# Mixture-of-experts stage: first weights split behind the weighing of the tile two back, and ahead of a one-tile expert's second weights

## What is computed

```
logits = flat @ router_w.T;  topk_w, topk_ids = top_k(softmax(logits), 4)
xs = rows of flat, sorted by expert            # 4096 tokens x 4 choices
gu = ragged_dot(xs, w1, group_sizes)           # w1: 32 x 1024 x 1024
act = silu(g) * u
ys = ragged_dot(act, w2, group_sizes)          # w2: 32 x 512 x 1024
routed = sum over the 4 choices of weight * ys
out = residual + routed + silu(flat @ sg) * (flat @ su) @ sd
```

## Time and profile before

| | |
|---|---|
| Median of three runs | 4691.68 us (4690.73 to 4694.3) |
| The profiled execution, its own time | 4695.12 us |
| Its span, first to last instruction | 4693.4 us |
| Mean granted TensorE clock | 0.978 |
| PE busy | 4473.3 us |
| DVE busy | 2569.9 us |
| ACT busy | 1795.0 us |
| POOL busy | 703.4 us |

### The profile page before, as it was taken

The page is one execution under the profiler, slowest core; times in us unless marked ns, Lnnn a source line. Parts: engine busy times, 40 slices in busy tenths (PEclk is TensorE's granted clock), DMA queues, the critical chain, the costliest instruction groups (busy, mean ns, idle before and its releaser), DMA issues.

```text
span 4693.4 us, 60863 instructions
## 1 busy us (share of the span) xinstructions
PE 4473.3 (95%) x19860; PEld 3545.8 (76%) x19863; DVE 2569.9 (55%) x2765; ACT 1795.0 (38%) x2596; POOL 703.4 (15%) x934
## 2 busy tenths in 40 slices
PE   6677999999999999999999999999999999999998
PEld 2245877777777777878888887887888878888787
DVE  8999999999999653433333434444341243333432
ACT  5665555555555332222222323334231242222321
POOL 1000000000000017111111111111111111111111
PEclk8888999999999999999999999999999999999999
DMA  6664866767676766654344545555452264444532
GB/s 227 248 255 177 292 237 249 261 225 272 246 264 232 263 219 185 242 180 114 99 127 112 165 116 161 169 163 188 141 170 58 59 202 128 112 112 116 161 108 62
DMA packets 247927, 835.08 MB, mean 178 GB/s; under 512 B 28160, under 2 KB 61056, under 8 KB 222976
## 3 DMA queue, kind: packets, MB, share of 16 engines
q1 hardware_dynamic: 172944, 572.77, 34.0%
q0 software_dynamic: 47728, 160.07, 15.4%
q10 hardware_dynamic: 27136, 100.67, 5.6%
HBM read 652.40 MB, written 181.01 MB: 178 GB/s over the span
## 4 chain that ended last, share of the span: by engine, by line
PE 85%; DVE 8%; issue 3%; ACT 3%; DMA 1%; DVEq 0%; ACTq 0%; POOL 0%; SPq 0%; POOLq 0%
PE ps L1545 35%; PE ps L1409 24%; PE ps L1559 17%; PE ps L1478 3%; PE ps L1431 1%; PE ps L1534 1%; DVE work L925 1%; DVE work L931 1%; PE ps L1419 1%; PE ps L1429 1%; DMA out<-work 1%; DVE work L952 1%; DVE work L954 1%; DVE work L935 1%; DVE work L958 1%
## 5 line engine op out<-in xcount | busy, mean ns | idle before, releaser
L1545 PE MATMUL ps<-halves 128*128 128x512 f32 x7152 | 1700.8, 394 | 25.8 <-DVE halves L1304 22.3
L1545 PEld LDWEIGHTS ps<-halves 128*128 128x128 f32 x7152 | 1340.0, 189 | 303.7 <-DVE halves L1304 24.4
L1409 PE MATMUL ps<-halves 128*128 128x512 f32 x6144 | 1451.5, 396 | 12.3 <-issue 12.3
L1409 PEld LDWEIGHTS ps<-halves 128*128 128x128 f32 x6144 | 1155.3, 189 | 285.7 <-issue 47.4
L1559 PE MATMUL ps<-halves 128*128 128x512 f32 x3576 | 834.9, 389 | 1.3 <-DVE halves L1324 1.3
L1559 PEld LDWEIGHTS ps<-halves 128*128 128x128 f32 x3576 | 671.2, 188 | 140.8 <-DVE halves L1324 1.6
L1308 DVE TENSOR_TENSOR halves<-ps,halves 128x1024 fp32r<-128x1024 f32 x150 | 183.6, 1224 | 884.4 <-ACT halves L807 884.4
L1304 DVE TENSOR_TENSOR halves<-work,halves 128x1024 fp32r<-128x1024 f32 (+1 forms) x320 | 440.5, 1433 | 114.9 <-ACT halves L811 114.9
L807 ACT ACTIVATE halves<-ps 128x1024 fp32r<-128x1024 f32 x150 | 154.0, 1027 | 849.6 <-PE ps L1545 849.6
L811 ACT ACTIVATE halves<-work 128x1024 fp32r<-128x1024 f32 (+1 forms) x320 | 369.7, 1221 | 96.3 <-PE ps L1559 66.5
L1324 DVE TENSOR_TENSOR halves<-ps,halves 128x256 fp32r<-128x256 f32 x298 | 112.3, 418 | 494.8 <-ACT halves L839 494.8
(11 more groups left out here) (186 smaller groups left out, 3787.8 us busy)
## 6 DMA issues: line engine op xcount, KB each, us to landing
halves<-split_dram SPq DMA_DIRECT2D x512, 512.0 KB, 5.6
work<-expert_w SPq DMA_DIRECT2D x192, 1024.0 KB, 5.7
split_dram<-halves ACTq DMA_DIRECT2D x32, 1024.0 KB, 4.9
plain<-shared_w SPq DMA_DIRECT2D x32, 512.0 KB, 3.2
gated_dram<-work ACTq DMA_DIRECT2D x32, 512.0 KB, 4.2
work<-side_t ACTq DMA_DIRECT2D x32, 512.0 KB, 5.5
work<-x_t ACTq DMA_DIRECT2D x32, 512.0 KB, 3.3
ratio_dram<-work ACTq DMA_DIRECT2D x32, 512.0 KB, 5.0
```

Of the source, the lines that this page charges most:

```text
L1409: last = pe.matmul(bank(k % 4), w, op[:, part], start=(c == 0 and w is w_hi and op is hi), stop=(c == CB - 1 and w is w_lo))
L1545: last = pe.matmul(ps_h[:, a * 512:a * 512 + 512], xp[:, xk * P:(xk + 1) * P], wp[:, rhs], start=(xk == 0 and xp is xhi and wp is whi[q]), ...
```

## The change

ACT and DVE use a new loop, `expert_loop_split`, in which `head` is taken apart into `first_weights`, `second_weights` and `rest` (a tile without its weighing). PE keeps `expert_loop`. The order on ACT and DVE becomes:

- expert e with more than one tile: `rest` of its first tile, its second weights, its other tiles, then the weighing of the tile two before the next expert's first, then the first weights of expert e+1. Before, those first weights came ahead of that weighing. Expert 0 ends in the same way.
- expert e with one tile: `rest` of its tile, then the first weights of expert e+1, then the weighing, then its own second weights. Before: its own second weights, the first weights of expert e+1, the weighing.

The counters of the splits are divided into one for first and one for second weights (8 and 2 steps for each expert) so that the two can be waited for in either order, on SP and PE too. DVE waits at the end of its opening tile until the last stores of the stage before have landed (`o_out`).

```diff
--- before.py
+++ after.py
@@ -28,7 +28,7 @@
...
-PIECES = 10
+W1, W2 = 8, 2
...
@@ -303,6 +303,48 @@
...
+        def expert_loop_split(eng, opening, weigh, rest, first_weights, second_weights, close):
+
+
+            def tile(g, j):
+                if not (isinstance(g, int) and g < 2):
+                    weigh(g - 2)
+                rest(g, j)
+
+            eng.wait_ge(s["cols_set"], 1)
+            opening(0)
+            tile(1, 0)
+            end0 = eng.value_load(cuts[0:1, 0:1], min_val=0, max_val=ROUTED_TILES - 2) + 2
+            with eng.If(end0 > 2):
+                with eng.Fori(2, end0) as g:
+                    tile(g, 0)
+            weigh(end0 - 2)
+            first_weights(1, end0)
+
+            with eng.Fori(1, EXPERTS - 1) as e:
+                first = eng.value_load(cuts[0:1, ds(e - 1, 1)], min_val=0, max_val=ROUTED_TILES - 2) + 2
+                end = eng.value_load(cuts[0:1, ds(e, 1)], min_val=1, max_val=ROUTED_TILES - 2) + 2
+                rest(first, e)
+                with eng.If(first + 1 < end):
+                    second_weights(e, first)
+                    with eng.Fori(first + 1, end) as g:
+                        tile(g, e)
+                    weigh(end - 2)
+                    first_weights(e + 1, end)
+                with eng.Else():
+                    first_weights(e + 1, end)
+                    weigh(end - 2)
+                    second_weights(e, first)
+            last = EXPERTS - 1
+            first = eng.value_load(cuts[0:1, last - 1:last], min_val=0, max_val=ROUTED_TILES - 2) + 2
+            end = eng.value_load(cuts[0:1, last:last + 1], min_val=1, max_val=ROUTED_TILES - 2) + 2
+            rest(first, last)
+            second_weights(last, first)
+            with eng.If(first + 1 < end):
+                with eng.Fori(first + 1, end) as g:
+                    tile(g, last)
...
@@ -475,7 +517,10 @@
...
-                    sp.wait_ge(s["w_lo"], (j - 1) * PIECES + (2 * q + 3 if q < 4 else q + 6))
+                    if q < 4:
+                        sp.wait_ge(s["w1_lo"], (j - 1) * W1 + (2 * q + 3))
+                    else:
+                        sp.wait_ge(s["w2_lo"], (j - 1) * W2 + (q - 2))
...
@@ -849,19 +894,18 @@
...
-            def tile(g, j):
-                if not (isinstance(g, int) and g < 2):
-                    weigh(g - 2)
+            def rest(g, j):
                 split_act(g - 1, 0)
                 split_act(g - 1, 1)
                 silu(g, 0)
                 split_x(g + 1)
                 silu(g, 1)
 
-            def head(g, j):
+            def first_weights(j, g):
                 for q in range(4):
                     split_weights(j, q, g)
-                tile(g, j)
+
+            def second_weights(j, g):
                 split_weights(j, 4, g)
                 split_weights(j, 5, g)
...
@@ -871,7 +915,7 @@
...
-            expert_loop(sc, opening, head, tile, close)
+            expert_loop_split(sc, opening, weigh, rest, first_weights, second_weights, close)
...
@@ -1300,8 +1344,12 @@
...
             def split_part_lo(j, q, i):
                 part = parts(q)[i]
-                ve.wait_ge(s["w_hi"], j * PIECES + (2 * q + i + 1 if q < 4 else q + 5))
-                ve.tensor_tensor(wlo[q][:, part], staged(q, part), whi[q][:, part].bitcast(f32), ALU.subtract).then_inc(s["w_lo"], 1)
+                if q < 4:
+                    ve.wait_ge(s["w1_hi"], j * W1 + (2 * q + i + 1))
+                else:
+                    ve.wait_ge(s["w2_hi"], j * W2 + (q - 3))
+                ve.tensor_tensor(wlo[q][:, part], staged(q, part), whi[q][:, part].bitcast(f32), ALU.subtract)\
+                    .then_inc(s["w1_lo" if q < 4 else "w2_lo"], 1)
...
@@ -1333,20 +1381,20 @@
...
-
-            def tile(g, j):
-                if not (isinstance(g, int) and g < 2):
-                    weigh(g - 2)
+                ve.wait_ge(s["o_out"], 16 * HALVES * CB + 1)
+
+            def rest(g, j):
                 split_act(g - 1, 0)
                 split_act(g - 1, 1)
                 gate_up(g, 0)
                 split_x(g + 1)
                 gate_up(g, 1)
 
-            def head(g, j):
+            def first_weights(j, g):
                 for q in range(4):
                     split_weights(j, q)
-                tile(g, j)
+
+            def second_weights(j, g):
                 split_weights(j, 4)
                 split_weights(j, 5)
...
@@ -1356,7 +1404,7 @@
...
-            expert_loop(ve, opening, head, tile, close)
+            expert_loop_split(ve, opening, weigh, rest, first_weights, second_weights, close)
...
@@ -1538,7 +1586,7 @@
...
-                        pe.wait_ge(s["w_lo"], j * PIECES + (2 * q + k // 2 + 2))
+                        pe.wait_ge(s["w1_lo"], j * W1 + (2 * q + k // 2 + 2))
...
@@ -1550,7 +1598,7 @@
...
-                    pe.wait_ge(s["w_lo"], j * PIECES + (q + 10))
+                    pe.wait_ge(s["w2_lo"], j * W2 + (q + 2))
```

More of the change, by code:

```diff
@@ L209, in adaln_moe @@
             "a_hi_s a_lo_s o_tr o_copy o_out prep prep_act masks rt rt_act rt_mask rt_pe cnt_copy "
-            "fill_set fill_out add_idx_set apart entry_ready listed_in slots_in cols_set w_hi w_lo w1_read w2_read "
+            "fill_set fill_out add_idx_set apart entry_ready listed_in slots_in cols_set w1_hi w1_lo w2_hi w2_lo w1_read w2_read "
             "rows_in row_idx_set x_tr x_hi x_lo silu_done act_done a_tr a_hi a_lo y_hi y_lo y_out zero_set "
@@ L218, in adaln_moe @@
         ONE_AHEAD = (
-            "o_tr o_copy o_out gated w_lo num ratio ratio_out gated_out a_tr w1_read w2_read act_done x_lo y_lo y_hi"
+            "o_tr o_copy o_out gated w1_lo w2_lo num ratio ratio_out gated_out a_tr w1_read w2_read act_done x_lo y_lo y_hi"
         ).split()
@@ L305, in expert_loop @@
                         tile(g, e)
+            close(eng.value_load(cuts[0:1, EXPERTS - 1:EXPERTS], min_val=1, max_val=ROUTED_TILES - 2) + 1)
+        def expert_loop_split(eng, opening, weigh, rest, first_weights, second_weights, close):
[34 more added lines that the diff above has]
+                    tile(g, last)
             close(eng.value_load(cuts[0:1, EXPERTS - 1:EXPERTS], min_val=1, max_val=ROUTED_TILES - 2) + 1)
@@ L810, in split_part_hi @@
                 sc.wait_ge(w_in[q], (j + 1) * 16)
-                sc.activation(whi[q][:, part], staged(q, part), ACT.Copy).then_inc(s["w_hi"], 1)
+                sc.activation(whi[q][:, part], staged(q, part), ACT.Copy).then_inc(s["w1_hi" if q < 4 else "w2_hi"], 1)
             sc.wait_ge(s["consts_in"], 64)
```

## The result

| | before | after |
|---|---|---|
| Median of four runs | 4692.73 us | 4824.44 us (4820.19 to 4828.56) |
| Span of the profiled execution | 4693.4 us | 4819.8 us |
| Ratio, 95% interval | | 1.0282, 1.027 to 1.0294 |
| Routed part: first product of tile 0 to the end | 2689.6 us | 2813.4 us |

The change costs 131.7 us in the medians (forecast 121) and 126.4 us in the two spans, 123.8 of them in the routed part, which runs from 2003.84 us in the kernel before and from 2006.43 us in the changed one. Lines have moved: L1593 is the first product (L1545 before), L1607 the second (L1559), L1351 DVE's weight splits (L1304), L856 ACT's (L811), L1378 and L890 the weighings, L1526 the transposes of the gathered rows.

The account below looks back on a forecast made before the run. TensorE was taken to bound the kernel, busy 95% of the span. Stalls 94.5 + clock 56.7 - one-tile saving 29.5 = +121.7 us on the profiled run gave 4816.8, forecast 4813 us for the median, range 4785 to 4852.

Parts of the forecast that it names:

- The cause and the sign: Whole kernel: PE waits at 27 reordered changes outweigh the one-tile saving; +121.7 us, slower with chance 0.97.
- The stall, 3.5 us, 27 times: At 27 changes of expert PE waits for weighing, then ACT's and DVE's first split: 3.5 us each, 94.5 in all.
- The clock, 2.1 us each: After each of the 27 stalls PE runs at lowered granted clock: 2.1 us, mean 1.5 to 2.7; 56.7 in all.
- The one-tile expert, 29.5 us saved: At four one-tile experts PE's wait for next first weights and its clock loss go: 7.4 us each, 29.5 in all.
- the 0.5 us at the second product: One-tile expert's second product: a new PE wait of some 0.5 us for late second weights, too short to lose clock.
- Edits at nothing: Weight loads on SyncE, GpSimd's adds and DVE's new store wait: side effects of the reordering, taken to cost nothing.
- The rival for this case: One-tile experts: no saving, as weight loads land late or the wait moves to the second product; 4843 us, chance 0.07.
- The sum: Whole kernel: 94.5 + 56.7 - 29.5 = +121.7 us, forecast 4813 us, +2.6%.
- The clock did not hold: Rival at the 27 changes: stalls too short or scattered to lower PE's clock; +65, 4757 us, chance 0.05.
- no wait for splits was longer than 3.3 us: Rival at the 27 changes: weighing also waits for an add and gain registers, so longer stalls; 4865 us, chance 0.05.
- no part but the one-tile branch got faster: Rival: PE can start before the first splits are done, so only the one-tile saving counts; 4662 us, chance 0.02.
- DVE's new wait for the last store: End of DVE's opening tile: taken as covered by tile 1's matmuls; uncovered it would cost a few us once.

Follow-up runs that it names:

- e1: Changed kernel with the 27 other changes of expert back in the old order, only the one-tile branch reordered: 4683.95 us against 4692.47 before, ratio 0.9983.
- e2: Changed kernel with the old order back in the one-tile branch, only the 27 changes reordered; another chip: 4955.98 us against 4822.93 before, ratio 1.0277.
- e6: Changed kernel with one half of the first weight group split ahead of the weighing at the 27 changes: 4892.82 us against 4822.93 before, ratio 1.0145.
- e11: The changed kernel run again unaltered on another chip, as yardstick: 4953.46 us against 4822.42 before, ratio 1.0261.
- e9: Kernel before, with only GpSimd's index copy moved ahead of its wait for the weighing: 4820.73 us against 4822.42, ratio 0.9998.

## Why the prediction was right, and where it was not

**The cause and the sign.** Right. The forecast was 4813 us, the measured median 4824.44, in the range. e1 and e2 take the change apart: the 27 reordered changes cost 133 us alone, the one-tile branch gains 8.5.

**The stall, 3.5 us, 27 times.** Measured 3.40 (PE's idle reads 3.23). The serial chain was as drawn; the 0.1 is ACT's split, which starts 0.59 us after the weighing's start and not 0.69. 27 x 3.40 = 91.8 against 94.5. e6 confirms the mechanism: one split taken out of the chain shortens each idle to 1.9 us.

**The clock, 2.1 us each.** The right mechanism, sized too high: 1.48, for the 27 39.8 us instead of 56.7, and just under the lower bound of 1.5 (e2 has 1.58, e11 1.77). I had taken the four idles of the earlier trace rows as typical and gave the idle that lost nothing too little weight; 5 of the 27 lost nothing. The sentence of the Trainium skill ("TensorE: Matmul & The Clock Gate", What's actually happening), by which the term would be left out, speaks of the ramp at the start of a kernel. The loss that the change added, 39.8 us, is indeed only 0.8% of the span, but it is 30% of the change's price; leaving the term out would have taken 56.7 us off a forecast that was already 11 low, and out of the range.

**The one-tile expert, 29.5 us saved.** This step failed: 8.5 us in e1. What it took away it took away as forecast (the 5.46 us waits are gone, and so is their clock), and the 0.5 us at the second product came out as nothing, since the splits began sooner than in the earlier trace rows. What failed are two terms put at nothing under "Edits at nothing". The first is that GpSimd's adds wait for weighings "which come sooner at the changes", as if that settled it. In the one-tile branch DVE's weighing did come sooner (6.45 us after PE's start, 7.8 before), but behind it stood the two second splits instead of activation splits that read PSUM; GpSimd was shut out, and the gather, which queues behind the add, went out 2.6 us later than before. The second is "the second weights' loads queue behind the first weights' on SyncE, as before": in the new order they hold up the loads behind them, which then go out in a crowd ahead of the gather, and its landing took 12.3 us instead of 6.3. Price: 4 x (4.1 + 1.7) = 23 us (3.9 of idle and 0.2 of lost overlap, as at the changes, and 1.7 of clock). The rival for this case had the full amount lost and looked for it in the weights' landing; it was the rows.

**The sum** in terms of the routed part: 91.8 + 39.8 - 31.5 + 23 = 123.1, measured 123.8, in one profile; with the clock of e11 the same sum is 8 us higher, and there the routed part took 134.6 us more than e9's. Two misses of opposite sign, some 20 us too much for the stalls and their clock and 21 too little for the one-tile experts, hid each other; the closeness of 4813 is in part luck.

**The other rivals.** The clock did not hold; no wait for splits was longer than 3.3 us; no part but the one-tile branch got faster. DVE's new wait for the last store shows no cost in the timeline; a kernel without it was not tried, since it protects the place that DVE's first weighing overwrites.

## What to carry to other kernels

In an in-order queue, an instruction that waits for the last thing an engine does must not stand ahead of what that engine needs next: the whole serial chain behind it becomes idle time, and here the clock added some 40% to that (39.8 us to 91.8). When an order is changed for a rare case, change it there alone (e1), and follow the moved work through every queue that waits for it, down to when the DMAs are let go. A wait that has two causes may be ended at the less obvious one; here that was the order of the loads in SyncE's queue.

## What the runs showed of the hardware

- GpSimd was held up while DVE's splits with two SBUF operands followed each other: a copy of 0.18 us took 4.10 and 8.64, the issue of an indirect DMA 4.92 instead of 1.58. The gap between two instructions of such a run let it in at times (0.83 us for the copy, 2.93 for the issue) and at times not.
- Idles of PE of 1.9 us cost granted clock at 12 of 27 places, idles of 3.2 us at 21 to 24 of 27, mostly 1.4 to 1.7 us or about 3.
- A gather of 128 rows landed in 12.3 us with six loads of 1 MB let go in the 6 us before it, in 10.2 and 8.4 with two, in 4.4 in the median.
- Three chips ran the part ahead of the routed experts some 125 us slower than another, the kernel before and the changed one alike, most of it in the stretch of the routing entries, where PE ran 47 matmuls in 120 us (e2); why was not looked into.
